# Table gathers no longer tied to products but each followed by a fill of an idle tile, five more product rounds summed by TensorE alone, and three units moved from VectorE to TensorE

## The reference

```python
e = jnp.stack([tbl_0[ids[:, 0]], ..., tbl_39[ids[:, 39]]], axis=1)      # (512, 40, 64)
i_idx, j_idx = np.triu_indices(40, k=1)                                  # 780 pairs
viW = jnp.einsum('bpd,pde->bpe', e[:, i_idx, :], W)                      # W: (780, 64, 64)
z = jnp.einsum('bpe,bpe->bp', viW, e[:, j_idx, :])
h = jnp.concatenate([z, dense_ctx], axis=1)
h = jnp.maximum(h @ W_top1 + b_top1, 0.0)      # 796 -> 512
h = jnp.maximum(h @ W_top2 + b_top2, 0.0)      # 512 -> 256
y = h @ W_top3                                 # 256 -> 1
```

## Time and profile before

| | us |
|---|---|
| median of 3 runs (lowest, highest) | 319.71 (319.37, 320.14) |
| profiled execution: its own time, as far as the page gives one, is its span | 361.1 |
| PE busy | 324.8 (90%) |
| DVE busy | 255.2 (71%) |
| POOL busy | 206.5 (57%) |
| ACT busy | 106.8 (30%) |

### The profile page before, as it was taken

The page is one execution under the profiler, slowest core; times in us unless marked ns, Lnnn a source line. Parts: engine busy times, 40 slices in busy tenths (PEclk is TensorE's granted clock), DMA queues, the critical chain, the costliest instruction groups (busy, mean ns, idle before and its releaser), DMA issues.

```text
span 361.1 us, 4423 instructions
## 1 busy us (share of the span) xinstructions
PE 324.8 (90%) x1700; PEld 115.7 (32%) x1700; DVE 255.2 (71%) x249; ACT 106.8 (30%) x266; POOL 206.5 (57%) x178
## 2 busy tenths in 40 slices
PE   7999739699888949949959999989999999999997
PEld 2444213133222313312312333333333333333455
DVE  5996535586676856945847899999999999990000
ACT  0216000060505551350767653025049000001032
POOL 3887737354735625634654538989987677770000
PEclk9999988899989969987998999999999999999999
DMA  7941212112212272302211346867798766650000
GB/s 170 337 154 51 60 32 66 43 47 73 57 42 53 78 257 92 79 21 52 73 51 42 81 86 147 176 145 158 151 193 172 170 136 118 117 109 9 15 0 0
DMA packets 17772, 35.34 MB, mean 98 GB/s; under 512 B 3924, under 2 KB 4952, under 8 KB 17624
## 3 DMA queue, kind: packets, MB, share of 16 engines
q0 software_dynamic: 7408, 16.26, 23.4%
q1 hardware_dynamic: 7848, 13.96, 12.9%
q10 hardware_dynamic: 2496, 4.84, 3.9%
HBM read 22.86 MB, written 0.00 MB: 63 GB/s over the span
## 4 chain that ended last, share of the span: by engine, by line
PE 59%; DVE 19%; issue 8%; POOL 6%; another core or an unknown queue 6%; DMA 1%; ACT 0%; DVEq 0%; POOLq 0%
PE y_ps L664 33%; PE z_ps L687 15%; DVE prod L558 14%; PE y_ps L697 4%; POOL prod L378 3%; POOL gathered L349 2%; DVE prod L484 2%; PE t_ps L697 2%; PE y_ps L743 1%; PE t_ps L571 1%; POOL prod L374 1%; DMA lane_rows_sb<-lane_rows 1%; DVE zT L494 1%; DVE x_quad L490 1%
## 5 line engine op out<-in xcount | busy, mean ns | idle before, releaser
L664 PE MATMUL y_ps<-x,w 64*128 64x512 f32 x780 | 190.0, 619 | 29.6 <-DVE prod L558 21.9
L349 POOL DMA_INDIRECT gathered<-in_tbl,ids_sb x128 | 131.2, 1025 | 94.6 <-DVE prod L558 55.9
L558 DVE TENSOR_TENSOR prod<-y_ps,x 128x1024 f32<-128x1024 f32 x89 | 103.8, 1216 | 54.8 <-PE y_ps L664 27.5
L664 PEld LDWEIGHTS y_ps<-x,w 64*128 64x128 f32 x780 | 70.6, 189 | 146.6 <-issue 104.0
L558 DVE TENSOR_TENSOR prod<-y_ps,x_quad 128x1024 f32<-128x1024 f32 x96 | 110.6, 1215 | 3.8 <-PE y_ps L664 1.9
L687 PE MATMUL z_ps<-prod,select 128*32 128x512 f32 x596 | 81.7, 652 | 1.2 <-POOL prod L378 1.2
L417 ACT COPY x<-x_fold 32x128 f32<-32x128 f32 x176 | 52.0, 295 | 84.2 <-DVE x_fold L527 70.6
L378 POOL TENSOR_TENSOR prod<-prod 128x1024 f32<-128x1024 f32 x23 | 55.3, 2406 | 0.8
L374 POOL DMA_DIRECT2D prod<-prod x23 | 21.6, 939 | 22.4 <-DVE prod L558 16.3
L687 PEld LDWEIGHTS z_ps<-prod,select 128*32 128x32 f32 x596 | 15.3, 114 | 59.4 <-issue 39.5
L440 ACT COPY x_mix<-x 64x512 f32<-64x512 f32 x40 | 24.7, 616 | 0.7
(11 more groups left out here) (47 smaller groups left out, 84.8 us busy)
## 6 DMA issues: line engine op xcount, KB each, us to landing
w<-w_rows SPq DMA_DIRECT2D x48, 256.0 KB
prod<-prod POOLq DMA_DIRECT2D x23, 512.0 KB, 4.6
gathered<-in_tbl,ids_sb POOLq DMA_INDIRECT x128
w<-w_rows ACTq DMA_DIRECT2D x1, 1792.0 KB
prod<-in_tbl ACTq DMA_DIRECT2D x6, 256.0 KB
prod<-hot_ids SPq DMA_DIRECT2D x4, 256.0 KB, 3.9
prod<-in_tbl ACTq DMA_DIRECT2D x4, 128.0 KB, 3.3
w<-w_rows ACTq DMA_DIRECT2D x1, 512.0 KB
```

The lines of the kernel that those rows point to most:

```text
L349: nc.gpsimd.indirect_dma_start(gathered[:, slot, c, s * DIM:(s + 1) * DIM], None, tables[f][:, :], bass.IndirectOffsetOnAxis(ap=ids_sb[:, ...
L558: nc.vector.tensor_tensor(prod[:, d % PROD_SLOTS, :, :], y_ps[:, d % DUO_SLOTS, :, :], factor, ALU.mult).then_inc(prod_ready, 1)
L664: last = nc.tensor.matmul(y_ps[:, d % DUO_SLOTS, half, :], w[rows, r % W_SLOTS, d % ROUND, :], x[rows, units[half], :], start=True, stop=True)
```

## The change

- The first 100 gathers wait for no product. Each is followed on POOL by a zero fill of a tile `idle` (128 x 256 float32) that nobody reads; from the second on the fill waits for the one before (`idle_filled`).
- The other 28 gathers wait for products from round 24 to 34.
- The plan gives each free gather a due time in products, 1.1 products for a gather, and places the folds by these: `gather_due[n] = max(n - 13, 0) * 11 // 10`, and a fold's duo is the due time plus 2.
- Units 9, 10 and 11 are turned by PE just before first use (duos 38, 46, 56). Units 12 to 19 are folded by DVE ahead of duos 65, 74, 83, 92, 104, 116, 132 and 144 (before: 60, 68, 76, 84, 92, 100, 124, 144).
- Rounds 24, 26, 27, 29, 31 and 33 are summed by PE from four products (before: 29 alone).

```diff
--- before.py
+++ after.py
@@ -35,17 +35,16 @@
 QUADS = (UNITS - PAIRED) // 2
 BLOCK_ROUNDS = QUAD // 4
 
-GATHER_LEAD = 2
-FOLD_LEAD = 6
-
-FOLDED = range(9, 20)
+FOLD_LEAD = 2
+
+FOLDED = range(12, 20)
 INSIDE = 3
 
-GATHERED_FIRST = 16
-
-ROUND_GATHERS = [4] * 24
-LATE_GATHERS = [1, 1, 2, 1, 1, 3, 1, 2, 1, 2, 1]
-UNADDED = [29]
+GATHERED_FREE = 100
+LANDING = 4
+
+LATE_GATHERS = [4, 1, 4, 3, 1, 4, 1, 4, 1, 4, 1]
+UNADDED = [24, 26, 27, 29, 31, 33]
 
 
 def pair_index(i, j):
@@ -113,15 +112,15 @@
 
 
         parts = 2 * CHUNKS
-        after = [0] * GATHERED_FIRST
-        for r, count in enumerate(ROUND_GATHERS + LATE_GATHERS):
-            after += [max(ROUND * r - 1, 1)] * count
-        assert len(ROUND_GATHERS) == self.quad_start[0] + 1 and len(after) == parts * (UNITS - HOT_UNITS)
+        after = [0] * GATHERED_FREE
+        for n, count in enumerate(LATE_GATHERS):
+            after += [ROUND * (self.quad_start[0] + 1 + n) - 1] * count
+        assert len(after) == parts * (UNITS - HOT_UNITS)
         self.gather_after = after
-        for u in range(HOT_UNITS + GATHERED_FIRST // parts, UNITS):
-            assert after[parts * (u + 1 - HOT_UNITS) - 1] + GATHER_LEAD <= self.transposed_at(u)
-        for u in range(PAIRED, UNITS):
-            assert self.transposed_at(u) // ROUND + 2 <= self.quad_start[(u - PAIRED) // 2]
+
+        self.gather_due = [max(n - 13, 0) * 11 // 10 for n in range(GATHERED_FREE)] + [d + LANDING for d in after[GATHERED_FREE:]]
+        for u in range(FOLDED.start, UNITS):
+            assert self.transposed_at(u) < ROUND * self.first_round(u) + ROUND
 
     def mixed(self, u):
         return [(f"mix{n}", u - 3, u) for n in range(3)]
@@ -146,7 +145,7 @@
             return 0
         if u >= FOLDED.start:
 
-            gathered = self.gather_after[2 * CHUNKS * (u + 1 - HOT_UNITS) - 1] + FOLD_LEAD
+            gathered = self.gather_due[2 * CHUNKS * (u + 1 - HOT_UNITS) - 1] + FOLD_LEAD
             if u < FOLDED.start + INSIDE:
 
                 return gathered
@@ -223,6 +222,7 @@
         head = sb("head", [ROWS, M1 + M2 + M2 * QUAD])
 
         y_out = sb("y_out", [ROWS, BATCH // 4])
+        idle = sb("idle", [ROWS, 256])
 
 
         hot = [prod[:, n // 2, n % 2, :].bitcast(BF16) for n in range(PROD_SLOTS)]
@@ -270,6 +270,7 @@
         hot_picked = sem("hot_picked")
         w_loaded = [sem(f"w_loaded{s}") for s in range(W_SLOTS)]
         unit_gathered = [sem(f"unit_gathered{s}") for s in range(GATHER_SLOTS)]
+        idle_filled = sem("idle_filled")
         unit_transposed = sem("unit_transposed")
         unit_folded = sem("unit_folded")
         x_ready = sem("x_ready")
@@ -350,6 +351,11 @@
                     gathered[:, slot, c, s * DIM:(s + 1) * DIM], None, tables[f][:, :],
                     bass.IndirectOffsetOnAxis(ap=ids_sb[:, c, f:f + 1], axis=0),
                 ).then_inc(unit_gathered[slot], 16)
+                if g - first < GATHERED_FREE:
+
+                    if g > first:
+                        pool.wait_ge(idle_filled, g - first)
+                    nc.gpsimd.memset(idle[:, :], 0.0).then_inc(idle_filled, 1)
 
             first = 2 * CHUNKS * HOT_UNITS
             done = 0
```

## The result

The changed kernel takes 339.5 us, median of four runs (338.26 to 340.06), against 319.54 us before (319.13 to 320.14): a ratio of 1.0614, 95% interval 1.0587 to 1.0641. Slower, as forecast, and 2.3 us over the forecast of 337.2.

A forecast was written before the change was run, and what follows sets the result against it. The prediction took PE as the bound from first duo to last, with the profile's stalls excluded. Terms 9.0 + 2.0 + 4.2 + 2.0 - 1.2 + 1.5 = +17.5 us on 319.71 gave 337.2 us, range 326 to 346.

The forecast's parts named there:

- Late fold: Unit 15's fold moves from duo 84 to 92; DVE waits for ACT's copies at duos 93 and 94: +9.0 us.
- Clock: PE's granted clock falls after its standstills around duos 93 and 94, slowing its matmuls: +2.0 us, between 0 and 2.8.
- Five rounds: Five more rounds summed by PE from four products, 0.84 us each: +4.2 us.
- POOL's gap: PE's 1.16 us wait for POOL's add goes, as POOL has fewer adds in rounds 24 to 34: -1.2 us.
- Three units on PE: Units 9, 10 and 11: three times four transposes on PE, 0.65 us together for each four: +2.0 us.
- The fills' pace: Gather plus fill on POOL takes 1.4 us, making early units' last gathers just in time or late: +1.5 us, between 0 and 6.
- The free start: Gathers freed from products give nothing, since POOL is already unbroken behind its first gathers: 0 us.
- queued behind a fill are only gathers: On POOL, a fill's wait for the fill before holds up nothing, since a whole gather lies between them.
- Rival A: PE's stalls are the kernel's own and the fills cure them: faster, 316 us; chance 0.06.
- B: Late fold at duos 93 and 94 is covered, so its wait and clock terms go: 326.2 us; chance 0.08.
- C: Fills set the pace at 1.8 us per gather and fill; first half 20 us late: 356 us; chance 0.10.
- D: The whole change does not move the time, within 0.2% or 0.6 us; chance 0.02.

The follow-up runs named there:

- e1: Changed kernel with units 14 and 15 folded ahead of duos 76 and 84 again, nothing else: 327.69 us, ratio 1.0244.
- e11: The changed kernel, unchanged, profiled and timed once more: 338.46 us, ratio 1.0566.
- e2: Changed kernel without the 100 fills, gathers still free of the products: 336.87 us, ratio 1.0519.
- e4: Changed kernel with fills only behind gathers 16 to 99: 338.94 us, ratio 1.0564.
- e7: Kernel before with rounds 24, 26, 27, 29, 31 and 33 summed by PE instead of 29 alone: 323.52 us, ratio 1.0133.
- e6: Kernel before with units 9 to 11 transposed by PE instead of folded by DVE, other folds held: 321.54 us, ratio 1.0075.
- e3: Kernel before, waits for products kept, with a fill behind each of its first 112 gathers: 326.18 us, ratio 1.0192.
- e8: Kernel before with 112 gathers free from the start, no fills, folds held at their products: 319.45 us, ratio 1.0.
- e10: e8 with a fill behind each of the first 16 gathers alone: 321.67 us, ratio 1.0077.
- e12: Changed kernel without fills and with units 14 and 15 folded at products 76 and 84: 327.45 us, ratio 1.0225.
- e9: e8 with 120 gathers free, the last eight one to a round, and POOL adding every round: 317.58 us, ratio 0.994.

## Why the prediction was right, and where it was not

- **Late fold, 9.0 predicted: 9.06 measured.** Duo 93 waited 3.48 for 3.5, duo 94 for ACT's last copy; e1 took it away. The reading of the earlier trace rows carried the forecast.
- **Clock, 2.0 predicted: 0.92 in the first profile, 1.02 in e11, 1.20 in e2, 1.97 in e4.** In the first profile the low level lasted about 3 us and not the 6 of the earlier trace rows, and in them DVE was busy 2.93 of 3 us with products that had piled up, so that PE's slower matmuls held up little. In e4 it lasted over 5 us. The size belongs to the execution; 2.0 is its upper end here.
- **Five rounds, 4.2 predicted: 4.3**, and **POOL's gap, -1.2: -1.2** (e7 has both).
- **Three units on PE, 2.0 predicted: 2.1 (e6) to 2.4 (after).** The four transposes last 0.65 us, the round grows by 0.79; the row's length is not all that a step costs.
- **The fills' pace, 1.5 predicted: 0.** The pace of 1.44 was well placed, but the sum went wrong in its starting point. It took gather number 12 at 29.54 us, as in before, behind gathers that lasted up to 4.83 us; with fills behind them number 12 started at 24.69. Where the first gathers have no fills the term is real (1.80 in e4). The landing, put at 2 us, has a median of 2.5. The last gather that I feared for ended at 53.6 us and was wanted at 62.4, and with the table on time still only at 59.4 (e1). Where the plan is tighter the pace does cost (e3).
- **The free start, 0 predicted: 0** (e8).
- **The start, no term: 5.3 measured.** About 2.4 are the fills beside DVE's one-hot comparisons (e10), the rest the late landing of the first table, which e1's execution did not have. The step that failed is "queued behind a fill are only gathers": it asked who waits for the fill on its own engine, and not which engine shares something with it. The prediction had listed the fill's cost to POOL alone.

The total came out within 2.3 us because 1.5 and 1.1 too much (pace, clock) stood against 5.3 missing; that was luck, and by its terms the forecast was less good than by its sum. Rival A (316 us) fell with e3: slower with the fills, not faster. B (326.2) is what the change costs if the late fold is covered, and e1, where it is, took 327.69. C (356) did not come about, D neither.

The stalls that I counted as profiling's own, 41.9 us, were taken out rightly: no run holds them. But the sum left 1.9 us of them in, nearly all in the stall of the earlier trace rows: the span without stalls is 317.3 (e8), not 319.2. A span lies 1.8 us below the time of its own run (317.3 and 319.10 in e8), so that the agreement within 0.5 us, on which the case against rival A leaned, came of two errors that met. What makes the stalls is open. The rule of the Trainium skill (NOTIFIC — the notification-queue block, section 7.1) that the prediction set beside them was tested by no run, and a second profile of the same kernel without them says only that they need not come.

Open too: why the first table lands late in some executions, and whether the change makes this more frequent. The wait of over 2 us is in the profiles of after, e2, e4, e11 and e12, five of the six with the changed kernel's plan (e1 is the sixth), and in none of the eight built on the kernel before, where it was 0.52 at most. That speaks for the change having a part in it; how, no run shows.

## What to carry to other kernels

A unit's last preparation must end before its first user, and the way there is the whole chain behind the fold (here 13.2 us over DVE and ACT), not the fold alone; half of this loss could be read from one row of ACT. An idle engine's filler is not free where another engine's instructions get longer beside it (here 0.40 us for each fill): ask for each added instruction what runs beside it on other engines, at the start above all. And freeing an engine early pays only if the time saved is moved to where that engine is short: e9 spent it on sums, and that is the only gain here.

## What the runs showed of the hardware

- A fill of 128x256 fp32 on POOL took 0.33 us, and up to 0.50 us beside DVE's int16 to bf16 comparisons, which went from 0.41 us each (3.25 for eight) to 0.51 on average. DVE's fp32 products from PSUM were not touched.
- Behind a fill the next gather began 0.16 us later, behind a gather 0.30 us. So gather and fill take 1.44 us where a gather alone takes 1.25: the fill costs 0.19 (away from the start).
- A gather landed 2.5 us after its issue in the median, in the changed kernel between 2.3 and 6.5.
- PE's granted clock after a standstill was not the same in every execution. After 3.06 us it stayed at 1.00 in the changed kernel (and in e11), and was 0.50 in e2 and e4. After 4.78 us it was 0.52 for the next 3 us in the changed kernel; after 3.14 us in e4 it was 0.50 for 5 us.
